# Convolution 0's scaled input made by ScalarE instead of GpSimd, in a four-layer style-modulated convolution and LoRA kernel

## The reference

```
x = x + ffn_l(cond_l(x, cond))             # l = 0..3

cond_l: four modulated 1-D convolutions with 3 taps (same, upsample, same, downsample), for each sample:
    s = style @ mw.T + mb
    weight = SCALE * w * s ;  demod = rsqrt(sum(weight^2)) ;  out = conv(x, weight * demod) + b
ffn_l, rows of 512:  x @ W.T + bias, and a low-rank part
    l=0: one fixed sum of LoRA products      l=1: top-2 of 8 experts by softmax
    l=2: gate-mixed LoRA per batch           l=3: top-1 of 4 experts
```

## Time and profile before

| what | us |
|---|---|
| median of three runs | 1156.78 |
| the profiled execution | 1158.54 |
| its span | 1156.7 |
| busy: PE, DVE, POOL, ACT | 1101.9, 539.2, 509.2, 332.1 |
| granted TensorE clock, mean share of full speed | 0.994 |

### The profile page before, as it was taken

The page is one execution under the profiler, slowest core; times in us unless marked ns, Lnnn a source line. Parts: engine busy times, 40 slices in busy tenths (PEclk is TensorE's granted clock), DMA queues, the critical chain, the costliest instruction groups (busy, mean ns, idle before and its releaser), DMA issues.

```text
span 1156.7 us, 47306 instructions
## 1 busy us (share of the span) xinstructions
PE 1101.9 (95%) x22032; PEld 796.1 (69%) x22032; DVE 539.2 (47%) x1157; ACT 332.1 (29%) x705; POOL 509.2 (44%) x380
## 2 busy tenths in 40 slices
PE   5899999999999999999999999999998999999997
PEld 4456777777766777777667777677676776776765
DVE  5774555344544444544444354544333354443343
ACT  2323333133332223223223223323221223222221
POOL 2536736345634544355353551465444243654300
PEclk9999999999999999999999999999999999999999
DMA  5455300010514000002124000003223000001011
GB/s 148 172 193 175 114 3 2 3 47 22 202 58 147 3 3 3 2 3 103 75 75 148 4 3 2 3 2 103 76 75 109 5 3 3 2 3 75 3 38 37
DMA packets 22307, 64.92 MB, mean 56 GB/s; under 512 B 4768, under 2 KB 5856, under 8 KB 17888
## 3 DMA queue, kind: packets, MB, share of 16 engines
q1 hardware_dynamic: 20576, 61.50, 14.8%
q10 hardware_dynamic: 1536, 0.40, 0.2%
HBM read 44.07 MB, written 17.83 MB: 54 GB/s over the span
## 4 chain that ended last, share of the span: by engine, by line
PE 76%; DVE 13%; issue 2%; DMA 2%; ACT 0%; DVEq 0%
PE bank_a L1554 14%; PE bank_b L1554 14%; PE bank_a L108 10%; PE bank_b L108 9%; PE bank_a L91 5%; DVE y L1248 4%; PE bank_b L91 2%; PE bank_b L67 2%; PE bank_a L67 2%; PE bank_b L79 2%; PE bank_a L79 2%; DVE y3t_lo L1303 2%; DMA out_x<-out_tile 2%; PE bank_b L1512 1%; PE bank_a L1512 1%
## 5 line engine op out<-in xcount | busy, mean ns | idle before, releaser
L1120 POOL TENSOR_TENSOR xs<-x,tab 128x512 f32<-128x512 f32 x96 | 112.4, 1179 | 418.1 <-DVE x L1317 418.1
L1107 POOL TENSOR_TENSOR sums<-raw 128x896 f32<-128x896 f32 x62 | 128.5, 2094 | 73.8 <-ACT raw L1158 73.8
L108 PE MATMUL bank_a<-y,wv 32*64 32x256 f32 x4096 | 119.9, 380 | 3.5 <-issue 3.5
L108 PE MATMUL bank_b<-y,wv 32*64 32x256 f32 x4096 | 115.5, 375 | 2.8 <-issue 2.8
L1554 PE MATMUL bank_b<-w_hi,y3t_hi 128*128 128x512 f32 x256 | 106.2, 415 | 6.7 <-DVE y3t_lo L1303 5.1
L1554 PE MATMUL bank_a<-w_hi,y3t_hi 128*128 128x512 f32 x256 | 106.5, 416 | 4.0 <-DVE y3t_lo L1303 3.4
L108 PEld LDWEIGHTS bank_a<-y,wv 32*64 32x64 f32 x4096 | 94.5, 132 | 21.9 <-issue 6.8
L108 PEld LDWEIGHTS bank_b<-y,wv 32*64 32x64 f32 x4096 | 94.0, 130 | 18.2 <-issue 4.1
L1554 PE MATMUL bank_a<-w_lo,y3t_hi 128*128 128x512 f32 x256 | 101.1, 395 | 0.0
L1554 PE MATMUL bank_b<-w_lo,y3t_hi 128*128 128x512 f32 x256 | 100.8, 394 | 0.0
L1136 POOL TENSOR_TENSOR x<-x,ob 128x512 f32<-128x512 f32 x64 | 80.0, 1285 | 0.0
(11 more groups left out here) (320 smaller groups left out, 1963.3 us busy)
## 6 DMA issues: line engine op xcount, KB each, us to landing
w_hi<-w_scratch SPq DMA_DIRECT2D x9, 1024.0 KB, 5.8
w_lo<-w_scratch SPq DMA_DIRECT2D x9, 1024.0 KB, 8.2
x_in<-in_x SPq DMA_DIRECT2D x32, 256.0 KB, 4.3
out_x<-out_tile SPq DMA_DIRECT2D x32, 256.0 KB, 2.3
w_raw<-in_w SPq DMA_DIRECT2D x3, 1024.0 KB, 8.7
w_scratch<-w_hi SPq DMA_DIRECT2D x3, 1024.0 KB, 4.1
w_scratch<-w_lo SPq DMA_DIRECT2D x3, 1024.0 KB, 7.9
w_raw<-w_scratch SPq DMA_DIRECT2D x2, 1024.0 KB, 9.5
```

The lines of the kernel that those rows point to most:

```text
L108: last = pe.matmul(banks[b][2 * CH * h:2 * CH * (h + 1), HALF * u:HALF * (u + 1)], keep["wv"][rows, a, SPAN - q:SPAN - q + 2].rearrange("p ...
L1107: g_.tensor_tensor(sums[i][:], pairs[:, :, one[0], one[1]:one[1] + SPAN], pairs[:, :, other[0], other[1]:other[1] + SPAN], ALU.add).then_i ...
L1120: nc.gpsimd.tensor_tensor(xs[:, b, 1:LEN + 1], src[:, b], column(n, T_S, b).broadcast_to((P, LEN)), ALU.mult).then_inc(xs_ready, 1)
```

## The change

POOL's four `xs` instructions of every turn are gone, and ACT makes them: `scaled_input(n + 1)` stands in step n of ACT's list behind `adapter_turned(m)` and ahead of `weights_hi` and `evacuate_3(n)`. Each quarter is one activation (Copy with a scale for each partition) that reads x from SBUF. It waits for the same events: the residual of that quarter (or the load of x_in in layer 0), and conv0 of the phase before, which reads the old xs. POOL's x + bias overwrites the x that xs is made from, so it now waits for `xs_ready` of its quarter.

```
-                for b in range(ROWS if n > 1 else 0):
-                    if l:
-                        pool.wait_ge(x_ready, tiles(n - 2, b + 1))
-                    else:
-                        pool.wait_ge(x_loaded[b], 16 * (group(n) + 1))
-                    pool.wait_ge(c0_done, n)
-                    nc.gpsimd.tensor_tensor(xs[:, b, 1:LEN + 1], src[:, b], column(n, T_S, b).broadcast_to((P, LEN)),
-                                            ALU.mult).then_inc(xs_ready, 1)
...
                     for b in range(ROWS):
+                        pool.wait_ge(xs_ready, tiles(n, b + 1))
                         if l == 0 and n >= 2:
...
+            def scaled_input(n):
+                src = x[n % 2] if layer(n) else x_in
+                act.wait_ge(c0_done, n)
+                for b in range(ROWS):
+                    if layer(n):
+                        act.wait_ge(x_ready, tiles(n - 2, b + 1))
+                    else:
+                        act.wait_ge(x_loaded[b], 16 * (group(n) + 1))
+                    a.activation(xs[:, b, 1:LEN + 1], src[:, b], ACT.Copy, scale=column(n, T_S, b)).then_inc(xs_ready, 1)
...
                 adapter_turned(m)
+                if n + 1 < PHASES:
+                    scaled_input(n + 1)
                 if n in MADE_IN:
                     weights_hi(MADE_IN[n])
```

## The result

| kernel | median, us | runs | ratio to the kernel before, 95% interval |
|---|---|---|---|
| before | 1157.28 | 20 | |
| changed | 1159.95 | 20 | 1.0022 (1.0011 to 1.0032) |
| changed, second comparison | 1158.03 (before: 1156.92) | 12 (before: 35) | 1.0007 (0.9992 to 1.0023) |
| changed, third comparison | 1159.45 (before: 1158.22) | 12 (before: 35) | 1.0015 (0.9999 to 1.0031) |

The forecast was 1157.8, that is +1.0 us, in a range of 1154.6 to 1160.5. The measured 1159.95 lies in the range, 2.15 us above the forecast; 0.5 of that is the kernel before, whose median is 1157.28 in 20 runs and was 1156.78 in the three that the forecast started from. The change cost 2.7, 1.1 and 1.2 us in the three comparisons: the sign and the size's order were right, and the size was small by 0.1 to 1.7 us. Only the first interval excludes no change at all, and all three are far under 2%.

The account below looks back on a forecast made before the run. PE was taken to bound the kernel, busy 1101.9 of 1156.7 us. Late step starts (0.88 us, plus 0.1) made +1.0: 1159.5 profiled, 1157.8 for the runs, whose median is 1.76 lower; range 1154.6 to 1160.5.

Parts of the forecast that it names:

- xs is hidden, before and after: Between last residual and conv0 in every step: PE never waits for xs, with 5.4 us of slack in step 3.
- ACT instead of POOL, value 0: POOL loses 125 us of busy time, ACT gains some 65; both are off the chain, so no time changes.
- w_lo 0.22 us later: POOL's low parts in six made steps: w_lo starts 1.22 us behind the last residual instead of 1.00.
- Four steps, +0.88 us: Starts of steps 2, 4, 20 and 28: the DVE addition waits for later sums, costing PE 4 x 0.22 us.
- Step 7, put at 0.1: Start of step 7: conv0 itself was late by as much as the DVE addition, so only 0.1 us was charged.
- Step 12 was counted at nothing: Start of step 12: DVE idles 0.68 us for conv0 behind the addition, taken as cover, so value 0.
- The sign on step 4: Start of step 4's transposes behind conv0: 3.95 to 4.0 us would show the forecast right, 3.34 us rival A.
- rival A: DVE's waits for POOL on the path shrink at seven step starts: up to 2.3 us faster, 1154.5; chance 0.12.
- L1298 waits for the running POOL instruction: At step starts DVE's 128x16 addition is blocked until POOL's instruction ends; PE waited for it eight times, 5.3 us.
- Non-made steps gain 0, gating safe: Steps without new weights: PE gains 0; in layers 1 and 3 sums starts 1.3 us behind the gating chain, value 0.
- B: PE runs out of instructions at other moments, a new span over 8.5 us: +4.4 us, 1162.2; chance 0.10.
- C: In layers 1 and 3 sums blocks DVE's small gating operations: +10 to +33 us, upward of 1168; chance 0.04.

Follow-up runs that it names:

- e3b: Changed kernel with xs' last quarter written three times on ACT in the 20 steps without new weights; 1158.39 us, ratio 1.0009.
- e2: Changed kernel with POOL making xs again at the end of the ten made steps, ACT in the other 20; 1157.60 us, ratio 1.0004.
- e3: Changed kernel with xs' last quarter written twice on ACT in the six made steps not tied to w_sum; 1157.81 us, ratio 0.9992; repeated, 1156.76 us.
- e4: Changed kernel with each sums on POOL split into two instructions of half the size; 1155.93 us, ratio 0.9980.
- e1: Changed kernel with w_hi ahead of xs on ACT in steps 1, 3, 6, 11, 19 and 27; 1160.03 us, ratio 1.0016.

## Why the prediction was right, and where its sizes were off

*xs is hidden, before and after.* Right: no wait of PE or of the span's evacuation for ACT's xs; L1158 is released by PE with 3.9 us of idle time, where 4.6 was forecast. e3b adds 1.5 us in 20 steps for nothing.

*ACT instead of POOL, value 0.* Right. The durations were off. POOL lost 135 us and not 125, because 96 of its xs took 1.18 us in the mean and not the 1.04 of the one in the earlier trace rows: some were held up themselves, up to 1.92. And an xs activation takes 0.73 us and the next starts 0.63 behind it (454.97 - 454.34), where I took w_hi's 0.52 spacing. It reads a scale for each partition, which w_hi does not; that this is the reason wasn't tried.

*w_lo 0.22 us later.* The mechanism was right, the term mis-sized: 0.33 behind the start of xs (1.33 against 1.00), 0.11 more than forecast, which is the longer xs; less the 0.05 by which ACT starts sooner behind the residual, 0.28 is left. e2 takes the step back and gets 1.00 again.

*Four steps, +0.88 us.* The transposes came 0.28 to 0.29 us later in steps 2, 20 and 28, the same 0.28. Step 7, put at 0.1, started its product at 6.14 instead of 6.01. Step 12 was counted at nothing, because in the trace of before DVE had 0.68 us of cover there. That cover was no property of the step: the span ahead of it was 0.84 us too long by a stop of PE, which gave POOL a lead (e2, without that stop, starts step 12 at 5.82). In the changed traces the stop was elsewhere and step 12 lost 0.5. In turn step 4 was spared twice, each time behind a span of 7.8 us. So that the sum came near the measured size is partly luck: a missed 0.5 in step 12 against a step 4 that cost nothing. The five steps cost 1.1 us more in the profiled runs of the first two comparisons (185.8 against 184.6) and 1.9 in the third (186.5). That covers 1.1 to 1.9 of the 1.1 to 2.7 us of the runs; PE's waits for the ends addition grew by 1.7 to 2.2. Above that the traces offer only PE's stops, which move from run to run, and the rest stays open.

*The sign on step 4.* "The transposes of step 4 at 3.34" was to speak for rival A, and 3.95 to 4.0 for the forecast. Two of the three changed traces have 3.39 and 3.44, the third 4.06. Read alone, the first trace would have pointed to A, though its steps 2, 7, 12, 20 and 28 have 4.05 or 4.06. A sign that hangs on one step of one trace was badly chosen.

*L1298 waits for the running POOL instruction.* Shown: e3 makes POOL later and PE earlier, e4 makes the instruction shorter with the same effect. The Trainium skill ("SBUF — State Buffer", section "Who interferes with whom") says that a DVE instruction with two SBUF inputs and a GpSimd instruction that reads SBUF contend for a shared pair of ports, which is an exclusive lock. Here the trace agrees: the addition ends within 0.1 us behind the end of POOL's instruction in the steps shown above, whole or halved.

*Non-made steps gain 0, gating safe.* Right. L1303 takes 0.19 us in every step but those behind made ones and has a median of 191 ns, and the small gating operations a mean of 174 to 193 ns as before.

*Rival A* (faster by freeing the lock) fell: POOL's sums stayed where they blocked. DVE did get freer, 528.3 us busy instead of 539.2, and none of it was on the path. *B* (a new stop of PE) did not come true by its sign, a span over 8.5 us where there was none, but e1 is a case of its kind, with its place and price (3.7 us). Whether an old stop got longer isn't settled: step 24, whose span holds one, lasted 39.4, 36.8 and 39.8 us in the three changed traces against 37.4 before, and 36.8 to 39.9 in all twelve traces with xs on ACT, in part or in whole, against 37.3 and 37.4 in the two with xs on POOL. *C* fell. The upper end of the range was too low for what it claims to hold: B with a loss of 3 us would be 1160.8, not 1160.5.

## What to carry to other kernels

Work moved off a busy engine onto an idle one is not free if something on the idle engine now stands behind it and feeds the busy one: look at what the new order makes late, and by how much. Where two engines block each other for whole instructions, the phase between their lists counts more than the sum of their work; halve the long instruction on the side that blocks, and then look for the next operation with the same kind of operands: the same edit gained 2.1 and 3.9 us on the changed kernel and nothing on the one before. A piece of cover that rests on a stall elsewhere is not to be counted.

## What the runs showed of the hardware

- A 128x512 f32 activation from SBUF to SBUF with a scale for each partition took 0.73 us, without one 0.644; on POOL the same product took 1.04 undisturbed.
- A 128x16 addition with both inputs in SBUF took 189 ns alone and up to 1.78 us beside a POOL instruction of 2.1; in the steps shown it ended 0.04 to 0.1 us behind that instruction. DVE operations with one input in PSUM (L1322, 0.69 us) kept their duration beside POOL.
- Splitting POOL's 128x896 addition in two cost 0.3 us for a pair (4.43 us for four halves against 4.13).
- With the DMA engines at 0.99 for 4 us, PE stopped for 2.23 us in the middle of conv0 (e1), and the granted clock was 0.50 from 0.7 us behind the end of the stop, for 3 us. With them at 1.00 for 4 us during the product PE did not stop (the changed kernel).
